# Letting side transposes into products that have begun, and new orders for batches 1 to 6, in a Mamba and expert kernel on one core

## The reference

```python
xz = einsum('bld,ed->bel', hidden_states, in_proj_w)      # 512 -> 2 x 1024
x  = silu(causal_conv4(x) + conv_b)
dt_lo, Bmat, Cmat = split(einsum('bdl,kd->blk', x, x_proj_w))   # 32 + 16 + 16
delta = softplus(dt_lo @ dt_proj_w.T + dt_proj_b)
# over the 512 positions, 1024 channels, 16 states:
h   = h * exp(delta * A) + delta * B_t * x_t
y_t = sum(h * C_t, axis=-1)
x1  = layernorm(hidden + ((y + x * D) * silu(z)) @ out_proj_w.T)
top2 of x1 @ gate_w.T, softmax weights w
out = layernorm(x1 + sum_k w_k * (x1 @ expert_w[e_k].T + expert_b[e_k]))
```

## Time and profile before

| | us |
|---|---|
| median of three runs | 2307.29 (2303.93 to 2315.99) |
| the profiled execution | 2310.68 |
| its span, first to last instruction | 2308.4 |
| before the first scan | 56.1 |
| loop of batch 0, 1 | 252.7, 262.9 |
| loops of batches 2 to 6 | 265.7, 266.2, 266.6, 269.3, 269.7 |
| loop of batch 7, with its half steps | 285.1 |
| tail | 114.1 |

### The profile page before, as it was taken

How to read it: one execution, slowest core, us unless ns; L and a number is a source line. 1 busy time by engine, 2 the same in 40 slices (tenths; PEclk the granted TensorE clock), 3 DMA queues, 4 the chain that set the end, 5 groups by cost and what they waited for, 6 DMA issues and landing times.

```text
span 2308.4 us, 30421 instructions
## 1 busy us (share of the span) xinstructions
PE 2060.7 (89%) x8624; PEld 1225.8 (53%) x8624; DVE 2041.5 (88%) x2319; ACT 1573.2 (68%) x2818; POOL 1849.1 (80%) x1505
## 2 busy tenths in 40 slices
PE   8896779897989989999899999899898998879898
PEld 3444455555555655555555555555555555545453
DVE  5899999999998999899998999989998999988923
ACT  5758856786577866778577875778666885555522
POOL 2959997789897889879897889879897797685603
PEclk9896879898999999999999999999998999889999
DMA  5412142368554686457863687547854576494775
GB/s 173 171 56 82 38 141 78 124 201 265 187 137 130 222 284 168 132 174 233 276 145 113 193 275 226 130 156 230 284 147 128 165 246 233 132 277 156 253 275 117
DMA packets 222084, 412.78 MB, mean 179 GB/s; under 512 B 29880, under 2 KB 36152, under 8 KB 221920
## 3 DMA queue, kind: packets, MB, share of 16 engines
q1 hardware_dynamic: 180448, 322.36, 41.1%
q0 software_dynamic: 20496, 57.16, 12.4%
q10 hardware_dynamic: 20976, 31.33, 4.1%
HBM read 299.37 MB, written 85.72 MB: 167 GB/s over the span
## 4 chain that ended last, share of the span: by engine, by line
POOL 34%; PE 26%; DVE 15%; issue 12%; DMA 6%; ACT 6%; SPq 1%; DVEq 0%; ACTq 0%; POOLq 0%
PE bank L1131 19%; POOL hst L1655 17%; DVE hst L1713 6%; POOL first_dbu L1655 5%; PE hTp L1147 5%; DVE y L1695 3%; POOL delta L1638 2%; POOL u L1641 2%; DVE u L1733 2%; POOL u L1599 1%; DVE hst L1892 1%; DMA spare<-gate_scratch 1%; DMA Bbc<-b_scratch 1%; ACT dA L1526 1%; POOL sorted_tokens L1578 1%
## 5 line engine op out<-in xcount | busy, mean ns | idle before, releaser
L1526 ACT ACTIVATE dA<-delta,negA 128x512 f32<-128x512 f32 (+1 forms) x1146 | 715.3, 638 | 361.0 <-DVE hst L1713 294.7
L1655 POOL TENSOR_TENSOR hst<-u,Bbc 128x512 f32<-128x512 f32 x666 | 877.9, 1422 | 33.1 <-PE hTp L1147 32.7
L1713 DVE TENSOR_TENSOR_SCAN hst<-dA,hst 128x512 f32<-128x512 f32 x672 | 788.6, 1208 | 22.3 <-ACT dA L1526 18.2
L1147 PEld LDWEIGHTS hTp<-ident,hst 128*128 128x128 f32 x4096 | 518.0, 154 | 356.3 <-issue 166.6
L1147 PE MATMUL hTp<-ident,hst 128*128 128x128 f32 x4096 | 583.7, 296 | 134.2 <-DVE hst L1713 33.0
L1695 DVE SCALAR_TENSOR_TENSOR y<-hTp,Ct,y 128x1024 f32<-128x1024 f32 x463 | 585.5, 1265 | 48.0 <-PE hTp L1147 44.7
L1655 POOL TENSOR_TENSOR first_dbu<-u,Bbc 128x512 f32<-128x512 f32 x222 | 291.2, 1392 | 13.5 <-DVE hst L1713 11.7
L1713 DVE TENSOR_TENSOR_SCAN hst<-dA,first_dbu 128x512 f32<-128x512 f32 x224 | 265.3, 1210 | 10.9 <-ACT dA L1526 8.8
L1131 PE MATMUL bank<-wslot,hidT 128*128 128x512 f32 x512 | 246.0, 616 | 20.0 <-ACT zs L1445 13.7
L1131 PE MATMUL bank<-wslot,tokT 128*128 128x512 f32 x496 | 232.8, 598 | 7.9 <-ACT ysb L1488 3.9
L1131 PE MATMUL bank<-delta,tokT 128*128 128x512 f32 x480 | 225.0, 604 | 0.3 <-issue 0.3
(11 more groups left out here) (176 smaller groups left out, 2810.9 us busy)
## 6 DMA issues: line engine op xcount, KB each, us to landing
wslot<-in_w_expT SPq DMA_DIRECT2D x90, 1024.0 KB
Bbc<-b_scratch SPq DMA_DIRECT2D x113, 256.0 KB
wslot<-in_w_inT SPq DMA_DIRECT2D x26, 1024.0 KB
y<-scaled POOLq DMA_DIRECT2D x49, 512.0 KB, 5.4
zs<-sorted_tokens ACTq DMA_DIRECT2D x91, 256.0 KB
sorted_results<-ysb SPq DMA_DIRECT2D x90, 256.0 KB
res<-in_w_expT SPq DMA_DIRECT2D x18, 1024.0 KB
gate_scratch<-zs SPq DMA_DIRECT2D x64, 256.0 KB, 2.0
```

What stands on the lines that cost most here:

```text
L1147: mm = nc.tensor.transpose(hTp[q % 2][:, tok(j)], hst[n % 2][:, j, start:start + P], ident[:, :])
L1526: nc.scalar.activation(decay_of(step, halved), delta[w.odd][:, j, cols], ACT.Exp, scale=negA[:, j, n:n + 1]).then_inc(exp_done, 1)
L1655: nc.gpsimd.tensor_tensor(dbu_row(n, j), u[w.odd][:, j, :], Bbc[n % 2][:, :], ALU.mult).then_inc(dbu_done, 1)
L1713: nc.vector.tensor_tensor_scan(hst[n % 2][:, j, :], dA[j % 2][:, :], dbu_row(n, j), 0.0, ALU.mult, ALU.add).then_inc(scan_done, 1)
```

## The change

It has three parts. `Segment` now calls `plan` with `weave` true for every segment. The urgency tables of SEG_TWO and SEG_FULL are replaced, with a pace of 0.45 for 0.6 and 0.48 for 0.45. And `xproj` on ScalarE, in the planner's list, comes after the last `bias` on TensorE, as the kernel's own wait (`weights_cleared`) has it. No instruction is added or taken away; the orders on the engines change. Of the tables one is shown, the other is of the same kind.

```diff
@@ tasks @@
-        "xproj": [("pe", mm, [(("sig", ND - 1), "pool", 0.1), (("load_wx",), "sp", 5)]), ("act", 0.6, [(x, "pe", 0.1)]), ("sp", 0.5, [(x, "act", 0.1)])],
+        "xproj": [("pe", mm, [(("sig", ND - 1), "pool", 0.1), (("load_wx",), "sp", 5)]), ("act", 0.6, [(x, "pe", 0.1), (("bias", NT - 1), "pe", 0.1)]), ("sp", 0.5, [(x, "act", 0.1)])],
@@ class Segment @@
-        order, users, turns = plan(pieces, steps, pace, steps > STEPS)
+        order, users, turns = plan(pieces, steps, pace, True)
...
-SEG_FULL = Segment(by_urgency({"pp": 601, "sk": -728, "L0": 544, "L1": -443, "m0": -364, "m1": 319, "Zb": 489, "py": 206, "m2": -212, "pd": -190, "mb": -113, "m3": 283, "mw": -202, "ld": 659, "o0": 214, "o1": -22, "ln": -52, "sc": -284, "lx": 49, "px": -126, "ps": -323, "Za": -835, "E0": 141, "E1": 446}), 0.45, W_FULL + W_O + GAP + [experts(2, LATE)], [x[0] for x in W_L])
+SEG_FULL = Segment(by_urgency({"pp": 30721, "sk": -114710, "L0": -130578, "L1": 49061, "m0": 9446, "m1": 21557, "Zb": 123078, "py": 33602, "m2": -109935, "pd": -36938, "mb": 36586, "m3": 4047, "mw": 25978, "ld": -27917, "o0": -86179, "o1": 69778, "ln": 70430, "sc": 10095, "lx": 29613, "px": 48242, "ps": -7051, "Za": 7465, "E0": 74583, "E1": -53734}), 0.48, W_FULL + W_O + GAP + [experts(2, LATE)], [x[0] for x in W_L])
```

More of the change, by code:

```diff
@@ L446 @@
 SEG_PRO = Segment(by_urgency({"ZB": -95, "Z": 7, "lb": -12, "lW": 135, "px": 47, "ps": -104, "pp": 76, "sk": -47, "py": 6, "pd": 21}), 0.36, W_Z + W_X, W_Z)
-SEG_TWO = Segment(by_urgency({"py": -29, "Zb": -25, "m0": 265, "ld": -335, "o0": 167, "o1": 65, "ln": -114, "sc": -365, "mb": 157, "pd": -13, "lx": -74, "px": 177, "ps": -4, "m1": -115, "Za": 77, "m2": 120, "m3": -270, "mw": -224, "pp": -137, "sk": -196}), 0.6, W_TWO + W_O + GAP + [experts(2, LATE)], [x[0] for x in W_L])
-SEG_FULL = Segment(by_urgency({"pp": 601, "sk": -728, "L0": 544, "L1": -443, "m0": -364, "m1": 319, "Zb": 489, "py": 206, "m2": -212, "pd": -190, "mb": -113, "m3": 283, "mw": -202, "ld": 659, "o0": 214, "o1": -22, "ln": -52, "sc": -284, "lx": 49, "px": -126, "ps": -323, "Za": -835, "E0": 141, "E1": 446}), 0.45, W_FULL + W_O + GAP + [experts(2, LATE)], [x[0] for x in W_L])
+SEG_TWO = Segment(by_urgency({"py": 2837, "Zb": 19764, "m0": -19197, "ld": -12446, "o0": 23732, "o1": 25028, "ln": -29865, "sc": -17515, "mb": 23940, "pd": -10142, "lx": 22004, "px": 19785, "ps": 1956, "m1": 1600, "Za": -5346, "m2": -1500, "m3": -14844, "mw": 11867, "pp": -6558, "sk": 57618}), 0.45, W_TWO + W_O + GAP + [experts(2, LATE)], [x[0] for x in W_L])
+SEG_FULL = Segment(by_urgency({"pp": 30721, "sk": -114710, "L0": -130578, "L1": 49061, "m0": 9446, "m1": 21557, "Zb": 123078, "py": 33602, "m2": -109935, "pd": -36938, "mb": 36586, "m3": 4047, "mw": 25978, "ld": -27917, "o0": -86179, "o1": 69778, "ln": 70430, "sc": 10095, "lx": 29613, "px": 48242, "ps": -7051, "Za": 7465, "E0": 74583, "E1": -53734}), 0.48, W_FULL + W_O + GAP + [experts(2, LATE)], [x[0] for x in W_L])
 SEG_EPI = Segment(by_urgency({"lz": 40603, "L0": -12829, "ld": 40646, "oe": 12233, "of": 16632, "ln": 33996, "sc": 73192, "wt": 29729, "we": 74915, "w2": -44476, "ww": 1169, "nz": 36915, "bi": 37626, "L1": -79432, "EE": 6520, "EF": 74926, "h0": 35050, "h1": 50697, "h2": -41491, "h3": 21347, "hl": 31160, "hd": -8979, "m5": -77866, "m6": 34116, "hm": -64328}), 0.95,
```

## The result

| | kernel before | new kernel |
|---|---|---|
| median, us | 2311.64 (4 runs, 2303.93 to 2317.63) | 2360.57 (4 runs, 2355.64 to 2370.39) |
| profiled execution, its span | 2310.68, 2308.4 | 2355.64, 2353.5 |
| ratio, 95% interval | | 1.0219, 1.017 to 1.0268 |

What follows compares the result with a forecast made beforehand. Loops were taken as bound by VectorE (247.0 of 266.6 us) with TensorE as full (245.7); five loops -9.0, batch 1 -2, head +7.0, tail +0.6 gave -3.4 us, median 2304, range 2276 to 2332.

Steps and rivals of the forecast that it cites:

- batch 1: Loop of batch 1: a third of batch 4's wait gains, no added `place` cost; -2 us, ends -7 and +4.
- TensorE late: Rival, chance 0.22: added TensorE work in steps 32 to 63 is waited for at the sums; 2323 or 2339 us.
- Steps 48 to 79, waits -4.7: Batches 2 to 6, per loop: waits at `x` -3.0, `gate` -0.9, `est` -1.3, `place` following `count` +0.5 us.
- Late steps, waits -3.0: Batches 2 to 6, steps 80 to 127: TensorE loses 5.8 us of work, VectorE's waits fall from 6.7 to 3.7 us.
- waits at sums near 3: Sign that the forecast is right: VectorE's waits at sums in steps 80 to 127 come near 3 us.
- `gate`, "-0.9 of the 2.4": Steps 48 to 79: with no shares ahead of its small products, `gate`'s 2.4 us wait for TensorE falls by 0.9.
- `place`, +4.9 per loop: Batches 2 to 6: moved `place` meets a busy GpSimd and takes 6.5 us instead of 1.6; bounds 0 and +4.9.
- Head, +7.0: Before the first scan: `yinit` transposes between `xproj` shares delay `rows` by 9.0 us, first scan by 7.0; bounds +5, +9.
- Steps 0 to 47, +1.0: Batches 2 to 6: TensorE gets 3.9 us more work, VectorE is charged 1.0 us; ends 0 and 3.9.
- "Cheap `place`": Rival, chance 0.20: GpSimd stands during `place`, so the 4.9 us fall away in all five batches; 2279.5 us.

Runs made afterwards that it cites:

- g2: g1 with ScalarE's routing-weight copy earlier and, in batches 2 to 6, one `bias` addition behind each of steps 76 to 79; 2330.2 us, ratio 1.0077.
- e4: New kernel, order unchanged, with `gate`'s subtraction done in ScalarE's exponential and `place`'s counts, owners and rows in PSUM; 2340.2 us, ratio 1.0134.
- f1: e4 and further: no copy of the logits, no index search, `hit` and `past` read from PSUM; 2341.9 us, ratio 1.0154.
- h1: New kernel, but in head and tail transposes may break the eight-share projection only ahead of its last share; 2351.83 us (one execution), first scan at 57.3.
- g1: f1 with head and tail ordered without transposes put into a begun product; 2332.0 us, ratio 1.0094.
- f2: f1 with ScalarE's copy of the routing weights moved earlier in batches 2 to 6, right behind tap 7; 2344.3 us against 2341.9.
- f3: Kernel before the change with all of f1's small-instruction edits; 2308.0 us against 2311.0, ratio 0.9993.

## Why the prediction was wrong

**The step that failed: the waits that were to go, -4.7 in steps 48 to 79 and -3.0 in the late steps.** From the windows of the two profiles, in us:

| batches 2 to 6, five loops | my step | measured |
|---|---|---|
| VectorE's busy time | +24.5 | +36.0 |
| VectorE's stands | -33.5 | -4.5 |
| together | -9.0 | +31.5 |

The waits are 29.0 us of a miss of 48, longer instructions 11.5, the head 4.5, batch 1 2.9. So I had the mechanism that makes instructions longer, with one instruction forgotten, and had it wrong that waits would vanish: they moved. My rival "TensorE late", at 0.22, had the reason: they "move more easily than they vanish".

- **Steps 48 to 79, waits -4.7: it is -0.4 in batch 4.** The 3.0 us at `x` did go, apart from 1.4, and the wait at `gate` went from 2.4 to 0.5. The one at `est` did not halve (2.6 to 3.0), and 3.7 us at `bias` came. I had said where the four `bias` go and asked only what they cost VectorE, 2.6 us. Their products now come behind 6 us of stands of TensorE and run at the lower clock, with two side transposes between the second and the third. This clock was a term I did not have. By an estimate from rows at the higher clock (a product starts 0.96 us behind the one before, eight blocks 0.87 us, the last product ends after 1.1), the second product, the transposes and the third product would take 3.0 us instead of 5.8. No run kept the clock up, so what it costs the loop is not shown. g2 shows that the wait at `bias` alone is not the cost: without it TensorE's work is late one stretch on.
- **Late steps, waits -3.0: it is -0.6.** Parts came in time (5.5 to 0.9 us over the whole loop, more than I had hoped). But `Ct` and a scan wait 1.7 us in steps 80 to 87, and the sum in steps 104 to 111 waits 2.4 us for the adding DMA issued at 1366.2. That DMA took 9.5 us to land in batch 4, 10.7 in batch 2, and 8.7 at the same place of the kernel before. The indicator "waits at sums near 3" came true by name (TensorE) and false in total.
- **`gate`, "-0.9 of the 2.4": its own cost was left out.** I moved `gate` by 18 steps, priced its wait for TensorE (it fell by 1.9) and never asked of it what I had asked of `place`: what GpSimd does beside it. The earlier trace rows had the answer. `gap` costs 2.6 to 4.0 us more per loop, and 5.3 in batch 1, where `place` in turn got 2.8 cheaper. With `den` (1.27 against 0.84), VectorE's busy time of a loop grows by 6.2 to 8.4 us where I had 4.9. Freeing these instructions in both pieces gave back 20 of the 49 us (e4). Freeing more gave nothing more (f1).
- **`place`, +4.9 per loop: right in kind, too high.** 1.6 to 5.0 us is +3.4, with the same instructions long as in the earlier trace rows. The bound from the nearest row held. This hid part of the miss at `gate`.
- **Head, +7.0: right in kind, mis-sized.** It is +11.5. I had the cause, the second share behind `yinit0` (h1 confirms it). I priced share and transpose at 1.36 us from rows in which TensorE ran through one kind without a break; in turns a pair takes 1.59 (49.02 to 50.61). That makes 1.6 us over seven pairs. Another 1.7 came from the first transposes, share and transposes behind the 6.5-us stand, 4.1 us instead of 2.4 at a low granted clock. I had taken each duration from a row at full clock. The first `yinit` began 0.4 us later than I had it, and 0.7 us lie between the end of the first decay (66.95) and the scan, where I had none.
- **Steps 0 to 47, +1.0:** -1.0 in batch 4; a difference of 2 us in one loop is less than loops differ between executions.
- **Batches 2 and 3, 5 us longer than 4 to 6.** They have the longest `gap` (4.1) and a granted clock of 0.93 against 0.94 to 0.96. In e4, without `gap`, they run at 270.3 and 269.3 with 0.94 and 0.95; that is 6 to 7 us less, where VectorE's busy time fell by 4.2. In most kernels here the loops at the lower clock are the longer ones: in f1 269.9 at 0.95 and 275.7 at 0.93, in g1 268.1 at 0.96 and 276.2 at 0.93. Which of the two causes the other was not separated.
- **The rivals.** "Cheap `place`" is refuted. "TensorE late", which I gave 2323 or 2339, named the wrong sign at the sums (they wait less) but came near the right stretch: TensorE is what f1 ran into in steps 48 to 55. A rival with `gate` under the same lock as `place` would have given my forecast plus some 2.6 x 5, and was not there.

What stays open: g1 and g2 are still 19 to 21 us above the kernel before, all of it in batches 2 to 6. Of the 4.1 us per loop in g1, VectorE's busy time is 1.2 and its stands are 2.9. By stretch the stands grew most in steps 48 to 63, from 3.5 to 7.2 us; in steps 80 to 127 they grew by 1.5, and in steps 0 to 47 and 64 to 79 they fell by 1.3 and 1.0. In steps 48 to 63 TensorE has more to do than before (37.2 us in g1, 27.7 before). The loops of g1 also spend 30 us at the lower clock, on average, against 25 before. No run took TensorE's work out of those steps and none kept its clock up, so this share is argued and not shown.

## What to carry to other kernels

When a piece is moved, ask for each instruction in it, on each engine, what the neighbour on the shared memory does at the new place: a 0.15-us instruction stood for the whole run of the neighbour's work here. A wait that is removed in a kernel with two engines at 92% each is worth nothing until you have said what the other engine does in these microseconds; f2, g2 and f3 removed waits or work and the time stayed. And ask where TensorE will stand for microseconds: the work behind such a stand ran at half the clock in the head and at `bias`. A product that accumulates while its inputs are still being made hides its time only as long as nothing that needs the last input is put between its shares.

## What the runs showed of the hardware

- VectorE's instruction with both sides in SBUF does not only wait for the GpSimd instruction that is running: `gap` stood 5.48 us in batch 1, over four multiplications in a row (435.19 to 440.39), and 4.1 in batches 2 and 3 over three. It ended each time within 0.05 us of the last of them; in batches 2 to 6 what follows there on GpSimd is the issue of a gather. In `place` an instruction got its turn between any two multiplications. What decides which, no run tells. The Trainium skill, SBUF — State Buffer, in its section on the two separate sides, has the lock held for an instruction; by that alone `gap` would have stood for one multiplication, some 1.2 us (an estimate; `begin`, held by one, took 1.20).
- Who was held: TENSOR_TENSOR (`gap`, 0.15 to 5.48) and TENSOR_SCALAR (`den`, 0.13 to 4.92) with SBUF on both sides, and the small scan (`end`, 0.17 to 1.28 over all runs). Not held beside the same GpSimd work: TENSOR_REDUCE (`owner` 0.27, `place` 0.20), SCALAR_TENSOR_TENSOR with PSUM (`row`, 0.17), MAX8 and FIND_INDEX8 (0.18 at most), and in e4 and f1 any of them with an operand in PSUM (0.16 to 0.26).
- TensorE's granted clock in the head was 1.00 up to 40.4 us, fell to 0.50 (the lower of its two levels, 1.2 GHz) within the 6.5-us stand, and was 1.00 again from 47.3 on; transposes of four blocks took 1.12 and 1.02 us instead of 0.66. At `bias` it fell after stands of 2.5 us and, 1.0 us of work later, part of the 3.5, and stayed at 0.50 for 13.7 us although TensorE worked without a break from 1308.9 on; eight blocks took 1.97 us instead of 1.04.
